# A cross-attention and expert layer: the expert slots in fours, and the same slots as one pipeline across the fours

## The reference

```
scores = sigmoid(x @ W_gate_router)
_, sel = top_k(scores + expert_bias, 2)            # 2 of 8 experts for each token
h = silu(xr @ Wg[e]) * (xr @ Wu[e])                # 256 -> 192
routed = (h @ Wd[e]) * w                           # 192 -> 256
out = shared.at[tok].add(routed)
```

## Time and profile before

| what | us |
|---|---|
| median of 3 runs (lowest, highest) | 557.61 (554.56, 559.33) |
| the profiled execution: its time | 554.13 |
| its span in the trace | 552.0 |
| TensorE busy in the span | 491.0 (89%) |
| VectorE, ScalarE, GpSimd busy | 341.1, 241.2, 212.0 |
| mean granted TensorE clock, share of full | 0.975 |

### The profile page before, as it was taken

How to read it: one execution, slowest core, us unless ns; L and a number is a source line. 1 busy time by engine, 2 the same in 40 slices (tenths; PEclk the granted TensorE clock), 3 DMA queues, 4 the chain that set the end, 5 groups by cost and what they waited for, 6 DMA issues and landing times.

```text
span 552.0 us, 11065 instructions
## 1 busy us (share of the span) xinstructions
PE 491.0 (89%) x2898; PEld 283.2 (51%) x2899; DVE 341.1 (62%) x1056; ACT 241.2 (44%) x471; POOL 212.0 (38%) x182
## 2 busy tenths in 40 slices
PE   4968899999888988889999794999999999999991
PEld 3843344444444433334555342576676776667660
DVE  2996467777888688746858832255555555555551
ACT  0577788878777867664251110122222222222220
POOL 4113211211100852144235550056555546655554
PEclk9998999999999999999999999699999999999997
DMA  7949501111101311134165564256656746665554
GB/s 242 341 158 334 123 19 39 59 58 40 39 21 38 118 59 40 48 121 140 68 213 190 182 183 154 57 84 100 118 83 89 119 83 98 99 110 94 87 86 48
DMA packets 43638, 60.45 MB, mean 110 GB/s; under 512 B 6512, under 2 KB 34672, under 8 KB 42992
## 3 DMA queue, kind: packets, MB, share of 16 engines
q1 hardware_dynamic: 28704, 36.92, 22.4%
q0 software_dynamic: 14896, 23.08, 21.5%
HBM read 33.77 MB, written 29.39 MB: 114 GB/s over the span
## 4 chain that ended last, share of the span: by engine, by line
PE 59%; DVE 17%; ACT 8%; DMA 7%; issue 6%; SPq 2%; POOLq 1%; DVEq 0%; POOL 0%; ACTq 0%
PE bankS L1065 15%; PE bankS L1081 10%; PE bankV L904 5%; PE bankS L998 5%; DMA out<-VR,attn 4%; PE bankR L760 4%; ACT attn L622 3%; PE bankV L908 2%; PE bankQ L760 2%; DVE rec L1306 1%; PE bankS L1016 1%; PE bankD L1054 1%; PE bankQ L1072 1%; PE bankS L1013 1%; PE bankS L888 1%
## 5 line engine op out<-in xcount | busy, mean ns | idle before, releaser
L533 POOL DMA_INDIRECT out<-VR,attn x71 | 109.6, 1544 | 104.9 <-DVE VR L1545 56.9
L1065 PE MATMUL bankS<-experts,scores_in 128*128 x284 | 104.5, 502 | 1.2 <-issue 0.5
L478 POOL DMA_INDIRECT sorted_rows<-XR,route x64 | 63.2, 988 | 84.1 <-PE bankD L910 22.0
L622 ACT ACTIVATE attn<-bankS,bias 128x512 f32<-128x512 f32 x128 | 81.0, 681 | 10.2 <-PE bankS L876 10.1
L1081 PE MATMUL bankS<-experts,scores_in 96*128 x284 | 73.1, 380 | 0.0
L736 ACT ACTIVATE scores_in<-bankS 128x192 f32<-128x192 f32 x71 | 23.4, 330 | 108.7 <-PE bankS L1065 107.7
L1065 PEld LDWEIGHTS bankS<-experts,scores_in 128*128 128x128 f32 x284 | 52.2, 194 | 33.2 <-issue 9.8
L904 PE MATMUL bankV<-attn,VS 128*32 128x512 f32 x256 | 64.0, 623 | 5.3 <-DVE OTT L1308 5.3
L906 PE MATMUL bankD<-attn,ON 128*32 128x512 f32 x256 | 64.0, 623 | 0.0
L1530 DVE TENSOR_TENSOR scores_in<-scores_in,bankS 128x192 f32<-128x192 f32 x71 | 25.1, 354 | 51.7 <-ACT scores_in L736 51.5
L454 POOL DMA_DIRECT2D x_in<-in_xT x13 | 9.5, 734 | 118.3 <-PE bankQ L760 117.2
(11 more groups left out here) (267 smaller groups left out, 835.1 us busy)
## 6 DMA issues: line engine op xcount, KB each, us to landing
VS<-sorted_rows SPq DMA_DIRECT2D x72, 130.0 KB, 2.9
x_cols<-X2T SPq DMA_DIRECT2D x16, 256.0 KB, 2.0
out<-X SPq DMA_DIRECT2D x8, 512.0 KB, 4.2
x_in<-in_xT POOLq DMA_DIRECT2D x15, 256.0 KB, 3.9
scores_in<-x_cols SPq DMA_DIRECT2D x14, 256.0 KB, 3.2
experts<-in_wgu SPq DMA_DIRECT2D x2, 1536.0 KB, 10.3
X<-in_x SPq DMA_DIRECT2D x1, 2048.0 KB, 17.7
experts<-in_wd SPq DMA_DIRECT2D x2, 768.0 KB, 17.4
```

What stands on the lines that cost most here:

```text
L478: pool.indirect_dma_start(sorted_rows.rearrange("s p r -> (s p) r"), bass.IndirectOffsetOnAxis(ap=index, axis=0), rows, None, bounds_check ...
L533: pool.indirect_dma_start(out, bass.IndirectOffsetOnAxis(ap=dest[:, i:i + 1], axis=0), y_out[:, i % 4], None, bounds_check=B * N + SPARE - ...
L622: act.activation(Pb[:, u % 2, c, :], bankS[:, c % GH, :], ACT.Exp, bias=bias[:, b, GH * g + c:GH * g + c + 1] if c < GH else biasR[:, b, g ...
L1065: last = pe.matmul(gate_bank(k)[:, 0:2 * F], x_col[:, k, c * P:(c + 1) * P], rhs, start=(c == 0), stop=(c == KC - 1))
```

## The change

The expert stage no longer drains at the end of a four. In every four each up is followed by the turn of the slot before it and by the down of the slot two before it, also where these belong to the four before (`earlier`). The transposes of the next four's first pair move from after down 1 to the place after the second up group (k = 1), those of the second pair to the end. VectorE goes in the same rhythm (inner k, columns k-1, result k-2), with `places` of the next four at the four's end. `h_col` and `y_out` are indexed modulo four. ScalarE copies the turned rows of a pair after its silu 1 and silu 3. Each `expert` number is read just ahead of its up, and since a register does not outlive a loop body here, the numbers of the two slots carried over are read again at the body's start.

```
 TensorE, four(a)
-                    e_ = [expert(4 * a)] + [None] * 3
+                    e_ = {k: expert(4 * a + k) for k in ((-2, -1) if earlier(a) else ())}
                     for k in range(tiles_):
+                        e_[k] = expert(4 * a + k)
                         up(k, e_[k])
-                        if k < tiles_ - 1:
-                            e_[k + 1] = expert(4 * a + (k + 1))
-                        if k >= 1:
+                        if k >= 1 or earlier(a):
                             turn(k - 1)
-                        if k >= 2:
+                        if k >= 2 or earlier(a):
                             down(k - 2, e_[k - 2])
-                    if more(a, tiles):
-                        transposes(a + 1, 0)
-                    turn(tiles_ - 1)
-                    down(tiles_ - 2, e_[tiles_ - 2])
-                    if more(a, tiles):
-                        transposes(a + 1, 1)
-                    down(tiles_ - 1, e_[tiles_ - 1])
+                        if k % 2 == 1 and more(a, tiles):
+                            transposes(a + 1, k // 2)
+                    if not more(a, tiles):
+                        turn(tiles_ - 1)
+                        down(tiles_ - 2, e_[tiles_ - 2])
+                        down(tiles_ - 1, e_[tiles_ - 1])
 VectorE, four(a)
-                    inner(0); inner(1); columns(0); inner(2); columns(1); result(0)
-                    inner(3); columns(2); result(1); columns(3); result(2)
+                    for k in range(tiles_):
+                        inner(k)
+                        if k >= 1 or earlier(a):
+                            columns(k - 1)
+                        if k >= 2 or earlier(a):
+                            result(k - 2)
                     if more(a, tiles):
                         places(a + 1)
-                    result(3)
+                    else:
+                        columns(tiles_ - 1)
+                        result(tiles_ - 2)
+                        result(tiles_ - 1)
 ScalarE, gates(a)
-                    if more(a, tiles):
-                        columns(a + 1)
+                        if k % 2 == 1 and more(a, tiles):
+                            columns(a + 1, k // 2)
```

More of the change, by code:

```diff
@@ L79, in of_four, with earlier @@
     return min(4, USED - 4 * a) if isinstance(a, int) else 4
+def earlier(a):
+    return not isinstance(a, int) or a >= 1
 def more(a, tiles):
@@ L721, in _, with columns @@
                 act.activation(late_r[:, k], late_r[:, k], ACT.Exp, scale=-0.5).then_inc(l_or, 1)
[L722 to L728, removed]
+            def columns(a, h):
+                act.wait_ge(f_xt["e"], 2 * a + (h + 1))
+                act.activation(x_col[:, 2 * h:2 * h + 2], row_bank(h).rearrange("p (t c) -> p t c", t=2), ACT.Copy) \
+                    .then_inc(f_xc["e"], 1)
             def ffn(kind, tiles):
@@ L733, in gates @@
                         act.wait_ge(f_gu[kind], 4 * a + (k + 1))
-                        if not isinstance(a, int) or a >= 1:
+                        if earlier(a):
                             act.wait_ge(f_h[kind], 4 * a + (k - 3))
                         act.activation(act_g[:, k], gate_bank(k)[:, 0:F], ACT.Silu).then_inc(f_si[kind], 1)
-                    if more(a, tiles):
-                        columns(a + 1)
+                        if k % 2 == 1 and more(a, tiles):
+                            columns(a + 1, k // 2)
                 return gates
@@ L749, in _ @@
                 shared(a)
-            columns(0)
+            columns(0, 0)
+            columns(0, 1)
             quads(act, SLOTS, ffn("e", SLOTS))
@@ L1076, in down @@
                         pe.wait_ge(f_hc[kind], 4 * a + (k + 1))
-                        if k >= 2 or not isinstance(a, int) or a >= 1:
+                        if not isinstance(a, int) or 4 * a + k >= 2:
                             pe.wait_ge(f_yd[kind], 4 * a + (k - 1))
@@ L1080, in down @@
                             rhs = wd_sb[0:FP, c, ds(e_, 1), :].rearrange("p o d -> p (o d)")
-                            last = pe.matmul(down_bank(k), h_col[0:FP, k, c * P:(c + 1) * P], rhs,
+                            last = pe.matmul(down_bank(k), h_col[0:FP, k % 4, c * P:(c + 1) * P], rhs,
                                              start=(c == 0), stop=(c == FC - 1))
@@ L1535, in columns @@
                         aside(dve)
-                        dve.tensor_copy(h_col[0:FP, k], (bankQ, bankR)[k % 2][0:FP, 0:D]).then_inc(f_hc[kind], 1)
+                        dve.tensor_copy(h_col[0:FP, k % 4], (bankQ, bankR)[k % 2][0:FP, 0:D]).then_inc(f_hc[kind], 1)
                     def result(k):
                         dve.wait_ge(f_y[kind], 4 * a + (k + 1))
-                        if not isinstance(a, int) or a >= 1:
-                            dve.wait_ge(y_st[k], BASE + 16 * a)
+                        if not isinstance(a, int) or 4 * a + k >= 4:
+                            dve.wait_ge(y_st[k % 4], BASE + 16 * (a + k // 4))
                         dve.wait_ge(e_dst, 2 * a + (k // 2 + 1))
@@ L1544, in result @@
                         w_k = w_slot[:, ds(4 * a + k, 1)]
[L1545 to L1560, removed]
+                        dve.tensor_tensor(y_out[:, k % 4], down_bank(k), w_k.to_broadcast([P, D]), ALU.mult).then_inc(f_yd[kind], 1)
+                    tiles_ = of_four(a, tiles)
+                    for k in range(tiles_):
+                        inner(k)
+                        if k >= 1 or earlier(a):
+                            columns(k - 1)
+                        if k >= 2 or earlier(a):
+                            result(k - 2)
                     if more(a, tiles):
                         places(a + 1)
-                    if four_:
-                        result(3)
+                    else:
+                        columns(tiles_ - 1)
+                        result(tiles_ - 2)
+                        result(tiles_ - 1)
                 return four
```

## The result

| | before | after |
|---|---|---|
| median, us (lowest to highest, 4 runs each) | 557.49 (554.56 to 559.33) | 582.23 (580.50 to 582.54) |
| span in the trace | 552.0 | 580.2 |

The ratio is 1.0463, 95% interval 1.0426 to 1.0501: 25 us slower. The forecast was 591, its range 577 to 605. Some executions of a kernel come out more than 1.5% longer than its fastest one, and every ratio and interval here leaves these out, while medians and ranges hold all runs.

A forecast was written before the change was run, and what follows sets the result against it. TensorE was taken to bound the expert stage, busy 10.64 of 10.69 us per four. Terms of +33.3, -4.76 and +6.7 gave +35.2 on 554.13, 589.3, set at 591 towards the runs' median; range 577 to 605.

The forecast's parts named there:

- part 1: Order of up, turn and down: turn 0's wait for inner, 0.10 us per four, goes; 1.7 us won at most.
- Part 3, the ring: First pair's transposes round through downs, result, `places` and row loads back to transposes: 12.80 us per four against 10.69.
- The landing: Ring's step from SyncE's second issue until the rows have landed: 2.9 us, rows showing 2.0 to 3.7.
- the step from landing to transposes: Ring's last step, a dispatch and a weight load ahead of the transposes: about 0.2 us.
- Part 2, the three loads: Three expert numbers read at the body's start: 1.5 us more sequencer work, hole 1.7 us at 17 crossings, alone +25.5 us.
- the lead there is much as before: At the loop's jump, the sequencer's lead over TensorE's queued work: 1.0 to 1.15 us.
- the second rival: Deep TensorE queue gives the sequencer a long lead, loads hidden, ring alone acts: about 577 to 580 us; chance 0.07.
- The sum: Expert stage: +33.3 us over 16 periods, -4.76 ahead of them, +6.7 behind; together +35.2.
- TensorE's own path per four is 12.2: TensorE's 10.38 us of work plus the jump's hole of 1.7 to 1.9, without waits for rows.
- Loads alone: Rows arrive in time, the three loads alone decide: +26 us, about 580 to 583; chance 0.14.
- Faster, both holes close: Both holes per four close, no new one opens: at most 5.3 us won, 549 to 552; faster or nothing 0.04.
- The clock: TensorE's clock falls to 1.2 GHz once per four: +44 us on top, 635; chance 0.05.

The follow-up runs named there:

- experiment 3: The changed kernel with the edits of experiment 1 and experiment 2 together; 553.04 us over ten runs, ratio 0.9918 to the kernel before.
- experiment 1: The changed kernel with `places` of the next four's first pair moved from the four's end to k = 1; 561.98 us, ratio 1.0127 to the kernel before.
- experiment 4: The kernel before, with only the transposes of the next four's first pair moved to k = 1, after turn 0; 606.91 us, ratio 1.0903.
- experiment 7: The changed kernel with the expert number for up 2 read ahead of the first pair's transposes; 574.81 us, ratio 1.0334 to the kernel before.
- experiment 8: Experiment 1 with the second pair's four transposes done twice, ahead of the jump, as dead work; 566.32 us.
- experiment 9: Experiment 5 with the second pair's transposes done twice in each four as dead work; 582.78 us, ratio 1.0486 to the kernel before.
- experiment 2: The changed kernel with the two carried slots' numbers read just ahead of their downs, one load at the jump; 587.65 us, ratio 1.0472 to the kernel before.
- experiment 5: The kernel before, with two more loads of an expert's number, unused, at each four's start from four 1 on; 593.36 us, ratio 1.0678.

## Why the prediction was right, and where it was not

**The bound and part 1** were read rightly: TensorE's work is 10.38 us per four, and experiment 3 runs at just that and wins the 5.3 us in the stage. The wait of turn 0 is gone after the change.

**Part 3, the ring**, was the right mechanism and, as forecast, the longer of the two. It waits in all 16 fours, removing it wins 19 to 20 us (experiment 1), making it alone costs 50 (experiment 4), and taking 0.5 us from one of its terms takes 4.9 us from the sixteen periods and 7.4 from the time (experiment 7). Its size was put 0.54 too high, 12.80 against 12.26, which is 8.7 of the sum. The landing was the mis-sized term: 2.9 was the median of all pairs before, while the three landings in the chain over 401 to 429 us of the changed kernel are 2.54, 2.29 and 2.73, and the 13 on the chain of the whole stage average 2.52. That is 0.38 of the 0.54. The second was the step from landing to transposes, 0.04 and not 0.2, the other 0.16. Why the landing is shorter stays open. The row loads share the DMA engines with the scatters of GpSimd, and the ring moves them against each other, but no run varied that alone.

**Part 2, the three loads**, has a right price and a wrong lead. Two more loads are 1.5 us of sequencer time: from the first load's start at 408.7 to the register step behind the third at 410.9 the changed kernel needs 2.2 us for three. The step that failed is "the lead there is much as before ... I take 1.0 to 1.15". The rows of the jump at 408.2 answer to the earlier trace rows:

```profile
L72 PEldq ALU_OP  x1: 32/32/32, 408.2 to 408.2; - x1
```

```profile
L1050 PEldq TENSOR_LOAD <-attn x3: 298/305/333, 408.7 to 410.3; - x3
```

The work queued then ends at 410.46: a lead of 2.26, and 0.65 of hole in place of 1.7. I had taken the 1.15 for the most that the sequencer can be ahead. It was the work behind the last wait that held it. Before, that was down 3's wait for columns 3, which VectorE finished at 412.50 + 0.42 = 412.92; the sequencer goes on at 413.0 (its row for L1081, below the VectorE row), reaches the jump at 413.2, and only down 3 and a few transposes are left to cover it.

```profile
412.50 0.42 DVE L1536 COPY scores_in<-bankR 96x256 f32<-96x256 f32 x1
```

```profile
L1081 PEldq FUSED_REGOPS  x2: 46/53/60, 413.0 to 413.1; - x2
```

In the changed kernel the last such wait is one slot further from the jump. With a lead of 2.26, the 2.85 us that the prediction reckons for the branch and three loads leave a hole of 0.59; measured is 0.65. Experiments 8 and 9 show it too: 0.43 us of work without a wait of its own, put ahead of the jump, shortens the hole by 0.43 us (0.62 to 0.19) and by 0.42 (1.87 to 1.45), and in 9 the lead grows from 1.16 to 1.56.

So the second rival had the queue right. By the page "TensorE: Matmul & The Clock Gate" of the Trainium skill (section "Architectural detail: the array is 16× 32×32, not 1× 128×128") TensorE's queue is 64 deep. At 408.2 in the changed kernel up 3's last passes, two of the turn, four of down 1 and four transposes were queued or running, a dozen, so the trace agrees with a long queue as far as it goes. My sentence that the trace does not agree with the page was wrong: a hole behind one load shows a late sequencer, not a short queue. But the rival's time, 577 to 580, rested on a hole of 0.2, and a sequencer that is held by waits still leaves 0.65.

**The sum**: +33.3, -4.8 and +6.7 were forecast; measured were +24.6, -4.8 and +5.6. The last is short by the hole's missing 1.05. "TensorE's own path per four is 12.2" was wrong too: with the ring away it is 11.1 (experiment 1). That did not enter the sum, since the ring was the longer either way.

**The rivals.** Loads alone is refuted by experiments 1, 2 and 4. "Faster, both holes close" is what experiment 3 does, after the ring and the loads are both undone, and its gain, 4.3 us in the medians and 5.3 in the stage, is what the prediction gave as the most a perfect pipeline wins, 5.3. (The landings of 0.7 us that the prediction asked for it go with a ring of 12.80; at the long lead that it also asks for, the ring is 12.16 and 1.3 would do. The fastest seen was 2.0, so nothing hangs on it.) The clock did not fall in the changed kernel (granted 1.00 over 362 to 565 us). The prediction argued from one hole of 1.64 that held; that was right for the changed kernel, whose idle time stands in three holes of up to about 1 us, and would have been wrong for the part alone.

## What to carry to other kernels

Moving a consumer forward in a software pipeline moves the deadline of the load that feeds it; follow the buffer's whole ring, release step included, and move the release with it. Ahead of a jump or a register load, count how much work without a wait is queued behind the last semaphore wait of the engine's sequencer: that, not the queue's length, is what covered it here. When two stalls overlap, removing one moves its time into the other, and one long hole can cost more than two short ones.

## What the runs showed of the hardware that was not expected

- A hole of 1.9 us in each period of 12.35 was followed by a fall of TensorE's clock to 1.2 GHz in 6 of 17 fours, at about 1.7 us each; a hole of 1.45 in a period of the same length was not, once (experiments 5 and 9). One hole of 1.62 us in experiment 2 was.
- A load of a register with the register steps behind it takes 0.65 to 0.75 us of TensorE's sequencer, of which the `TENSOR_LOAD` itself is 0.30; three in a row take 2.2 (408.7 to 410.9 in the changed kernel).
- A semaphore wait of TensorE's stream holds its sequencer too, so nothing behind it is prepared, not even register work that does not depend on it. In the changed kernel the register steps of the load for up 2 begin at 404.2 and 416.2, together with the transposes that waited for the rows (404.20 and 416.20), and before the change the last steps ahead of the jump begin at 413.0, when down 3's wait ends.
